# ScalarE's queue in place of SyncE's for the loads of x and the stores of y

## The reference

```python
def layer0(x, gn_w, gn_b, qkv_w, qkv_b, proj_w, proj_b):
    h = group_norm(x, gn_w, gn_b).reshape(B, C, H * W)        # 32 groups
    q, k, v = split(einsum('oc,bcn->bon', qkv_w, h) + qkv_b)
    attn = softmax(einsum('bcn,bcm->bnm', q, k) * C ** -0.5)  # 1024 x 1024 per image
    h = einsum('bcm,bnm->bcn', v, attn)
    return x + einsum('oc,bcn->bon', proj_w, h) + proj_b

def layer1(x, Wq, bq, Wk, bk, Wv, bv, gamma):
    q, k, v = Wq @ x + bq, Wk @ x + bk, Wv @ x + bv           # q and k have 16 channels
    attn = softmax(einsum('bdi,bdj->bij', q, k))
    return gamma * einsum('bcj,bij->bci', v, attn) + x
```

## Time and profile before

| | us |
|---|---|
| median of 3 runs | 1585.69 |
| lowest, highest | 1584.01, 1586.72 |
| the profiled execution | 1587.17 |
| its span, first to last instruction | 1585.0 |
| PE, DVE, ACT, POOL busy | 1483.5, 1284.3, 1214.9, 1238.6 |
| mean granted clock of TensorE | 0.987 |

### The profile page before, as it was taken

The page is one execution under the profiler, slowest core; times in us unless marked ns, Lnnn a source line. Parts: engine busy times, 40 slices in busy tenths (PEclk is TensorE's granted clock), DMA queues, the critical chain, the costliest instruction groups (busy, mean ns, idle before and its releaser), DMA issues.

```text
span 1585.0 us, 43920 instructions
## 1 busy us (share of the span) xinstructions
PE 1483.5 (94%) x16777; PEld 1120.0 (71%) x16777; DVE 1284.3 (81%) x2508; ACT 1214.9 (77%) x1698; POOL 1238.6 (78%) x1027
## 2 busy tenths in 40 slices
PE   5799999999999989999999999999999999999977
PEld 2567777767777767776777777777777677767756
DVE  6678888877888878887888888878888788878885
ACT  3578877877787878877878778878878788778874
POOL 4788878878888878787888878888888788788653
PEclk9899999999999999999999999999999999999999
DMA  1999999999999999999999999999999999999999
GB/s 49 164 164 195 202 200 197 203 193 202 187 203 203 202 197 200 196 195 200 206 196 200 202 194 200 202 200 198 201 196 198 206 193 199 197 199 195 191 194 183
DMA packets 1081438, 305.22 MB, mean 193 GB/s; under 512 B 1068272, under 2 KB 1068944, under 8 KB 1081232
## 3 DMA queue, kind: packets, MB, share of 16 engines
q1 hardware_dynamic: 1080080, 302.41, 110.2%
q10 hardware_dynamic: 1152, 0.00, 0.0%
HBM read 17.13 MB, written 16.78 MB: 21 GB/s over the span
## 4 chain that ended last, share of the span: by engine, by line
SPq 47%; PE 29%; DVE 7%; DMA 7%; ACT 5%; issue 4%; POOL 1%; DVEq 0%; ACTq 0%; POOLq 0%
SPq L304 44%; DMA pt<-rows 6%; PE mixed L816 4%; PE mixed L818 4%; PE mixed L817 4%; PE scores L771 3%; DVE nmax L565 3%; DVE rows L582 3%; PE scores L773 2%; PE scores L772 2%; PE scores L801 2%; SPq L295 2%; ACT rows L473 2%; PE bank_w L890 2%; PE bank_w L882 1%
## 5 line engine op out<-in xcount | busy, mean ns | idle before, releaser
L565 DVE TENSOR_REDUCE nmax<-scores 128x1 f32<-128x1024 f32 x512 | 620.4, 1217 | 149.8 <-PE scores L801 131.4
L816 PE MATMUL mixed<-v_head,pt 128*128 128x129 f16 x4096 | 719.6, 222 | 3.4 <-DMA pt<-rows 3.1
L817 PE MATMUL mixed<-v_tail,pt 128*128 128x128 f16 x4096 | 718.9, 219 | 0.0
L818 PE MATMUL mixed<-v_head,pt 128*128 128x129 f16 x4096 | 718.8, 220 | 0.0
L366 POOL TENSOR_TENSOR rows<-prob,rows 128x1024 f16<-128x1024 f32 x256 | 545.3, 2130 | 21.4
L361 POOL TENSOR_SCALAR rows<-prob 128x1024 f16<-128x1024 f32 x256 | 267.5, 1045 | 265.8 <-ACT prob L460 161.0
L465 ACT ACTIVATE scores<-scores,nmax 128x1024 f32<-128x1024 f32 x256 | 278.9, 1089 | 183.7 <-DVE nmax L565 183.1
L817 PEld LDWEIGHTS mixed<-v_tail,pt 128*128 128x128 f16 x4096 | 406.0, 99 | 3.1
L816 PEld LDWEIGHTS mixed<-v_head,pt 128*128 128x128 f16 x4096 | 399.5, 98 | 5.4 <-DMA pt<-rows 4.6
L818 PEld LDWEIGHTS mixed<-v_head,pt 128*128 128x128 f16 x4096 | 397.1, 97 | 0.0
L582 DVE SCALAR_TENSOR_TENSOR rows<-scores,rows 128x1024 f16<-128x1024 f32 x256 | 312.9, 1222 | 78.4 <-ACT rows L473 78.2
(11 more groups left out here) (110 smaller groups left out, 1923.0 us busy)
## 6 DMA issues: line engine op xcount, KB each, us to landing
x_raw<-in_x_dram SPq DMA_DIRECT2D x32, 512.0 KB, 4.6
out_dram<-y SPq DMA_DIRECT2D x64, 256.0 KB, 3.2
pt<-rows SPq DMA_TRANSPOSE x512, 5.1
w_qkv<-in_L_conv_qkv_w_dram SPq DMA_DIRECT2D x3, 64.0 KB, 4.1
b_qk<-in_L_conv_bk_dram SPq DMA_DIRECT2D x8, 0.1 KB, 2.3
b_qk<-in_L_conv_bq_dram SPq DMA_DIRECT2D x8, 0.1 KB, 1.9
w_proj<-in_L_conv_proj_w_dram SPq DMA_DIRECT2D x1, 64.0 KB, 4.9
w_v<-in_L_conv_Wv_dram SPq DMA_DIRECT2D x1, 64.0 KB, 4.7
```

Source lines behind the costliest of these rows:

```text
L565: nc.vector.reduce_max(nmax[l][:, tile.i % TILES:tile.i % TILES + 1], scores[l][:, :], AX.X, negate=True).then_inc(maxed[l], 1)
L816: mm(mixed[l][:, 0:C + 1], head, vh[:, p, m, 0:C + 1], start=(m == 0), stop=False)
L817: mm(mixed[l][:, 0:C], head, vt[:, p, m, :], start=False, stop=False)
L818: done = mm(mixed[l][:, 0:C + 1], tail, vh[:, p, m, 0:C + 1], start=False, stop=(m == TILES - 1))
```

## The change

The loads of x for the images 3 to 31 (29) and all stores of y (64) leave SP's queue and go to the end of ACT's body of the same slot. The load of image 3 moves from slot 0 to slot 3. SP keeps the weights, the loads of the images 0 to 2 and the 512 transposes.

```diff
-LOADS = Steps(-16)
-LOADS_LEFT = -11
+LOADS = Steps(-16, first={3: (-13,)})
@@ SP
             def body(slot):
-                for im, _ in LOADS.at(slot):
-                    load_x(im)
                 if tile := TILE_AT[0].get(slot - SWING[0]):
                     swing(tile)
-                for im, h in STORE.at(slot):
-                    store_y(im, h)
                 if tile := TILE_AT[1].get(slot - SWING[1]):
                     swing(tile)
...
-            every_slot(body, LOADS_LEFT)
+            load_first(2)
+            every_slot(body, 0)
@@ ACT
+            def load_x(im):
+                act.wait_ge(x_biased, im.n - X_BUFS + 1)
+                act.wait_ge(h32_done, im.n - X_BUFS + 1)
+                act.wait_ge(h_head_done, im.n - X_BUFS + 1)
+                act.dma_start(x_raw[:, im.n % X_BUFS, :], x_img[im.n]).then_inc(x_loaded[im.n % X_BUFS], 16)
+
+            def store_y(im, h):
+                act.wait_ge(y_done, im.n * TILES + PER_HALF * (h + 1))
+                act.dma_start(out_img[im.n, :, h * HALF:(h + 1) * HALF], y[:, h, :]).then_inc(y_stored[h], 16)
...
                 for im, _ in H_HEAD.at(slot):
                     h_head_out(im)
+                for im, _ in LOADS.at(slot):
+                    if im.at_least(X_BUFS):
+                        load_x(im)
+                for im, h in STORE.at(slot):
+                    store_y(im, h)
```

More of the change, by code:

```diff
@@ L284, in _, with load_first @@
             col = lambda v: v.rearrange("(p a) -> p a", a=1)
[L286 to L295, removed]
+            def load_first(n):
+                sp.dma_start(x_raw[:, n, :], x_img[n]).then_inc(x_loaded[n], 16)
             def swing(tile):
@@ L308, in body @@
             def body(slot):
-                for im, _ in LOADS.at(slot):
-                    load_x(im)
                 if tile := TILE_AT[0].get(slot - SWING[0]):
                     swing(tile)
-                for im, h in STORE.at(slot):
-                    store_y(im, h)
                 if tile := TILE_AT[1].get(slot - SWING[1]):
                     swing(tile)
-            load_x(Image(0))
+            load_first(0)
             for j in range(3):
                 sp.dma_start(w_qkv[:, j, :], qkv_w[j * C:(j + 1) * C, :]).then_inc(w_qkv_loaded, 16)
-            load_x(Image(1))
+            load_first(1)
             for dst, src in ((w_proj[:, :], proj_w), (w1_v[:, :], Wv), (w1_qk[0:CQK, :], Wq),
```

## The result

The changed kernel takes 1569.55 us (median of 5 runs, 1566.0 to 1575.75) against 1584.86 us (median of 5, 1581.39 to 1586.72). The ratio is 0.9918, 95% interval 0.9898 to 0.9937: 0.8% faster. The forecast was 1550 us, 2.2% faster. The sign and the range held; the size is less than half of what was forecast.

The account below looks back on a forecast made before the run. SP's queue of transposes and the ring of PE, DVE and ACT were taken as close rivals. From 1587.2 us, -6.4, -43.6, +11 and +3, less 1.5 for the median, gave 1550 us; range 1537 to 1602.

Parts of the forecast that it names:

- What bounds the kernel: Whole kernel: SP's queue issuing transposes and the engines are close rivals; late transposes cost 1.56 us per image, 43.6 over 28.
- The ring: PE, DVE and ACT working in turn: they need 46.25 us per image when nothing else is late, against 47.81 measured.
- The start, -6.4: First tiles: with image 3's load off SP, the first transpose goes some 13 us earlier and a 6.37 us wait disappears.
- ACT's issues, +3: ACT's queue in the middle: 93 added issues, stores covered by idle time, loads costing 0.1 us per image.
- the lock: Rival on ACT: descriptors made for one queue at a time, so ACT's issues wait for SP's transposes; 1600 us, chance 0.24.
- SP's queue in the middle, -43.6 + 11: SP's steady part: without 2.64 us per image of other work nobody waits, -43.6; a quarter of the cost left, +11.
- The test that the prediction had named: SP's steady part: the forecast is wrong if SP's time per transpose rises above 2.89 us.
- The stops: Transpose stream: moments when it nearly stands still, with no load or store beside; they stay, and some tiles still wait.
- Covered, but only just: DMA engines: five transposes leave 3.1 us of room for 2.7 us of load and first store.
- The engines stay full: Rival on the DMA engines: same bytes, so only the start gains; 1582 us, or 1568 with a third; chance 0.15.
- The ends of the forecast case: Total time: range 1538 to 1567 us, from no wait left to half of the 43.6 left and ACT at 6; chance 0.58.

Follow-up runs that it names:

- e1: The kernel before, all on SP, with loads of images 3 to 31 and all stores cut to 64 columns: 1540.09 us, ratio 0.9715.
- e2: The changed kernel, x and y on ACT, with loads of images 3 to 31 and all stores cut to 64 columns: 1532.00 us, ratio 0.9665.
- e3: The kernel before with only the load of image 3 moved from slot 0 to slot 3, still on SP: 1578.13 us, ratio 0.9960.
- e11: The changed kernel with only the loads of images 3 to 31 cut to 64 columns, stores whole: 1538.33 us, ratio 0.9690.
- e12: The changed kernel with only the stores cut to 64 columns, loads whole: 1533.90 us, ratio 0.9662.
- e5: The changed kernel with the loads of x on ACT four slots earlier from image 5 on: 1567.16 us, ratio 0.9896.
- e6: The kernel before, all on SP, with image 3's load at slot 3 and loads four slots earlier from image 5 on: 1576.19 us, ratio 0.9943.
- e8: The changed kernel with each load of images 4 to 31 cut into two halves, two slots apart from image 5 on: 1557.65 us, ratio 0.9834.
- e10: The kernel before, all on SP, with image 3's load at slot 3 and later loads in halves, two slots apart from image 5: 1589.84 us, ratio 1.0018.
- e13: The changed kernel with loads in two halves, issued one behind the other at one slot, four slots earlier: 1570.39 us, ratio 0.9906.
- e7: The changed kernel with loads on ACT four slots earlier and each image's first store one slot later: 1575.40 us, ratio 0.9932.

## Why the prediction was right and wrong

- *What bounds the kernel.* Right. The ring of 46.25 us per image is real: with small transfers (e1, e2) all 28 images take 46.0 to 46.4. And the 43.6 us above it are waits for transposes: they vanish in e1 and e2.
- *The start, -6.4.* Right in kind: the first transpose starts at 29.05, the third tile's head on ACT at 42.84 instead of 49.23, with no wait. By the image at 128.33 it had grown to 8.1; e3 has it alone.
- *ACT's issues, +3.* Too dear: they take 0.35 us, begin while an ACTIVATE runs, and cost 0: with small transfers the middle is 1294.9 with the 93 issues on ACT and without them (e2, e1). A mean issue of 1.3 us would have been needed for the lock.
- *SP's queue in the middle, -43.6 + 11.* This step failed, by its second term. 33.2 us were left, not 11. The argument was that a transpose at 215 GB/s leaves 0.62 us of engines that can do 288 GB/s, and that load and store would pass in this room. They don't fit into this room. In the windows of the changed kernel (columns as in rows 10) around the load that ACT issued at 703.88:

```profile
702.50:703.70 1.20, 1.20 (x16) 0.66 (x13) 0.52 (x3) 1.15 (x4) 0.81 (x1) 1.00 0.75 12
704.40:705.70 1.30, 1.30 (x11) 0.80 (x9) 1.30 (x2) 0.88 (x2) 1.30 (x1) 1.00 1.28 288
706.00:706.70 0.70, 0.70 (x16) 0.70 (x14) 0.70 (x1) 0.61 (x2) 0.70 (x2) 1.00 0.97 144
707.30:708.20 0.90, 0.90 (x19) 0.90 (x17) 0.90 (x3) 0.90 (x2) 0.82 (x3) 1.00 0.96 382
```

  Before the issue the stream stands nearly still (12 GB/s). The backlog then runs at 288 GB/s, falls to 144, and some 3 us after its issue the load's bytes move. At their densest the engines pass 382 GB/s, a rate that no stretch of transposes reached. The queues between 706.8 and 709.1 us (packets, MB, share as in rows 2; q10 carries the load, q1 the transposes):

```profile
q10 hardware_dynamic: 144, 0.52, 62.9%
q1 hardware_dynamic: 679, 0.17, 62.7%
```

  The load takes 2.3 us where the sum had 1.8, and beside it the transposes move 0.17 MB, or 75 GB/s in place of 215. Over the 29 loads the packets say the same: the first bytes move 1.1 to 3.2 us after the issue (median 2.1), and the transfer takes 2.4 us in the median. So the load does not fit into the room of the transposes but displaces most of them while it passes. SP's issues around it are long (chain of waits of the changed kernel: start, us, what):

```profile
702.28 3.41 SPq L295
...
705.88 3.77 SPq L295
```

  Only the second of them has the load's bytes in it; in the first lies the stop of 702.5. What the bytes cost in all is read from the whole run: the mean issue of a transpose is 2.34 us without them (e2) and 2.73 with them, which is 6.3 us of SP's time per image where the sum had 3.6 us of transfers (1.8 + 2 x 0.9) inside free room. The test that the prediction had named for this (a transpose above 2.89 us of SP's time) came out at 2.95.
- *The stops.* The prediction left them as they were, and it did not count what they take from the room. Between 100 and 1450 us the packets of the changed kernel show 121 stops of 0.8 us or more (under 40 GB/s), 158 us together, so over 5 us per image and more than load and stores take at 288 GB/s. Of these 117 begin within 1.2 us behind one of the 16 KB packets of the page's queue q8 ("instruction", 137 in the run). That these packets cause the stops was not tested. By themselves the stops make no tile late: e2 has 105 of them, and its middle is 1294.9.
- *Covered, but only just.* The sum of 3.1 us of room for 2.7 of transfer was too close to be taken as cover. e11 and e12 show a threshold: half of the bytes cost at most 1.2 us and all of them cost 33. A margin of 0.4 on a sum of rates read from two short windows should have split the chances evenly between the forecast and the rival.
- *Rivals.* "The engines stay full" named the cause and its time with a third of the gain (1568) was the result; it should have had more than 0.15. The range held because it was drawn wide enough to take in this rival, not because the sum was near. The lock did not show: issues on ACT are shorter beside transposes (0.35) than in the setup (0.45).
- *The ends of the forecast case.* By its own terms they are 1585.7 - 6.4 - 43.6 = 1536 and, with 21.8 and 6 added, 1564, and not 1538 and 1567. The forecast of 1550 doesn't hang on them.
- *Two queues, and the lock.* The Trainium skill (DMA: Bandwidth & Descriptors, "Issuing engines are not separate DMA queues") says that issuing from a second engine saves only the sequencer's time. The runs agree as far as they go: with small transfers and the start set aside the second queue is worth nothing (e2 against e1). With all bytes it is worth 6 us in the changed kernel (against e3), 9 us with the loads at - 20 (e5 against e6) and 32 us with halves (e8 against e10), so where SP is the bound its saved time is not small. The lock of the generator, which the Trainium skill has under Perfetto Trace Analysis, "DMA Instruction — HWDGE (DVE, Sync)", is not seen between the two queues: of the 93 ACT issues 84 begin while SP issues a transpose, and none takes over 382 ns. Only an issue directly behind another on ACT grows (e13), and whether the lock is at work there was not tried.

Left open: why the transposes slow to 144 GB/s before the load's bytes move, what stops the stream behind the packets of q8, and why quarters are no better than halves.

## What to carry to other kernels

Before moving DMAs to another queue, make their transfers small (same number, few bytes) in both places: that tells in two runs whether the bytes are what costs, and how much there is to win at all. It doesn't tell what an issue costs beside the full bytes: here it was nothing with small transfers, and 6 to 32 us lay between the queues with the full bytes. So compare the queues with the full bytes too. Where a stream of transposes is the bound, spread what else must pass in pieces over slots with slack, and issue these pieces from a queue that is not behind; on the queue that is behind, each piece adds its own issue. Keep the pieces apart: two halves at one place were no better than the whole, and two slots apart they won 12 us. Costs near a threshold don't add: two transfers that are each free can cost 33 us together.

## What the runs showed of the hardware that was not expected

- A DMA of 0.5 MB from a second queue, issued while transposes ran, did not share the engines with them evenly: it passed in 2.3 us, some 3 us after its issue, and the transposes moved 0.17 MB meanwhile (75 GB/s against 215).
- Nearly all stops of the transpose stream (117 of 121, 1.3 us each in the mean) follow a 16 KB packet of the queue q8.
- Issuing a load or a store took ACT 0.33 to 0.38 us in each of 93 cases, 84 of them while SP was in the middle of issuing a transpose, and in 92 it began beside an ACTIVATE. On SP, behind transposes, such an issue took 0.33 to 1.70 us. Directly behind another load on ACT (e13) it took 0.38 to 1.42 us, so what stands ahead in the same queue counts and not only which engine issues.
- A transpose's issue can grow to 7.7 us when such transfers come from the other queue (9.4 us in e7); the longest before was 5.0.
